# GpSimd's indirect DMAs in two expert layers, placed one or two slots apart

## The reference

```python
x = x + 0.5 * ffn0(layernorm(x))          # one 128x128 projection
x = x + linear_attention(layernorm(x))
x = x + 0.5 * ffn0(layernorm(x))
x = x + 0.5 * expert_layer(layernorm(x))  # <- the change is in this layer
x = x + attention_one_head(layernorm(x))
x = x + 0.5 * expert_layer(layernorm(x))  # <- and in this one

def expert_layer(src):                    # 16 heads of 8, 4 experts, ff 512
    q, k, v = src @ Wq + bq, src @ Wk + bk, src @ Wv + bv
    x = layernorm(src + softmax(q k^T / sqrt(8)) v @ Wo + bo)
    key = floor(x @ router_w + router_b) mod 4
    ff = relu(x @ W1[key] + b1[key]) @ W2[key] + b2[key]   # each token: one expert
    return layernorm(x + ff)
```

## Time and profile before

| what | value |
|---|---|
| time, three runs | 1491.17, 1488.88, 1481.77 us, median 1488.88 |
| the profiled execution, from its first to its last instruction | 1560.5 us |
| busy TensorE, VectorE, ScalarE, GpSimd | 1172.4, 944.3, 819.0, 691.4 us |
| mean granted clock of TensorE | 0.829 |
| chain that ended last | PE 53%, DVE 14%, issue 9%, DMA 7% |
| indirect DMAs on GpSimd | 64 scatters, 64 gathers, 48 weight transfers |

### The profile page before, as it was taken

One profiled execution on the slowest core, in us unless ns is written; L12 is line 12 of the kernel. 1 busy time (PEld: TensorE's weight loads), 2 busy tenths in 40 slices (PEclk: granted clock), 3 DMA queues, 4 the chain that ended last, 5 costly groups with the idle time before them and its releaser, 6 DMA issues.

```text
span 1560.5 us, 30073 instructions
## 1 busy us (share of the span) xinstructions
PE 1172.4 (75%) x10624; PEld 759.1 (49%) x10624; DVE 944.3 (61%) x2991; ACT 819.0 (52%) x1850; POOL 691.4 (44%) x679
## 2 busy tenths in 40 slices
PE   4899999874466987988886676467779888987753
PEld 3666766562133645644554564332326545644553
DVE  5477777664467656667526885556667566663231
ACT  4666555452165756765662343224557657754532
POOL 5335345465122454454427676442133544543352
PEclk8799999975588978979987988756869879887977
DMA  8000000002222433343112110202234433432133
GB/s 250 2 2 1 2 2 2 2 1 81 84 83 76 134 108 118 117 137 126 45 53 71 41 50 22 71 21 72 74 102 134 125 108 117 125 106 84 37 99 104
DMA packets 116340, 116.72 MB, mean 75 GB/s; under 512 B 9288, under 2 KB 100040, under 8 KB 116040
## 3 DMA queue, kind: packets, MB, share of 16 engines
q1 hardware_dynamic: 101488, 74.84, 15.4%
q0 software_dynamic: 11008, 36.81, 7.2%
q10 hardware_dynamic: 3696, 3.15, 0.7%
HBM read 73.01 MB, written 42.15 MB: 74 GB/s over the span
## 4 chain that ended last, share of the span: by engine, by line
PE 53%; DVE 14%; issue 9%; DMA 7%; ACT 6%; SPq 4%; POOL 4%; another core or an unknown queue 3%; ACTq 0%; POOLq 0%; DVEq 0%
PE bank L1657 7%; PE bank L1695 7%; PE bank L1672 6%; PE bank L1716 6%; DVE NM L2276 3%; DMA scr_m<-MH 2%; SPq L741 2%; PE bank L1904 2%; PE bank L1480 2%; PE bank L1745 2%; PE bank L1734 2%; PE bank L1806 2%; PE bank L1722 1%; PE bank L1422 1%
## 5 line engine op out<-in xcount | busy, mean ns | idle before, releaser
L2276 DVE TENSOR_REDUCE NM<-bank 128x2 f32<-128x512 f32 x512 | 340.1, 685 | 233.0 <-PE bank L1722 195.4
L1244 ACT ACTIVATE PBS<-bank 128x512 f32<-128x512 f32 x512 | 300.0, 604 | 263.5 <-PE bank L1716 222.3
L1716 PE MATMUL bank<-QS,KS 50*128 50x256 bf16 x1024 | 201.4, 300 | 129.1 <-DVE NM L2276 64.3
L874 POOL TENSOR_TENSOR rs<-ve,half 128x4 f32<-128x4 f32 x88 | 90.0, 1023 | 434.3 <-DVE ve L2187 329.6
L1722 PE MATMUL bank<-KS,QS 48*128 48x256 bf16 x1024 | 210.7, 310 | 27.0 <-DVE NM L2276 17.1
L1716 PEld LDWEIGHTS bank<-QS,KS 50*128 50x128 bf16 x1024 | 66.4, 98 | 261.6 <-issue 153.2
L1695 PE MATMUL bank<-PBS,V 128*32 128x256 f32 x2048 | 163.9, 446 | 1.4 <-ACT PBS L1244 1.4
L983 POOL DMA_INDIRECT scr_x<-XS,POS x64 | 63.9, 998 | 82.5 <-DVE POS L2242 63.5
L1722 PEld LDWEIGHTS bank<-KS,QS 48*128 48x128 bf16 x1024 | 66.0, 99 | 55.8 <-DVE NM L2276 40.6
L1695 PEld LDWEIGHTS bank<-PBS,V 128*32 128x32 f32 x2048 | 59.2, 121 | 63.8 <-issue 35.1
L1218 ACT ACTIVATE HB<-bank,W 128x128 f32<-128x128 f32 x256 | 74.5, 396 | 24.1 <-PE bank L1657 19.9
(11 more groups left out here) (319 smaller groups left out, 2672.8 us busy)
## 6 DMA issues: line engine op xcount, KB each, us to landing
QS<-scr_q SPq DMA_DIRECT2D x64, 192.0 KB
KS<-scr_k SPq DMA_DIRECT2D x56, 192.0 KB
XD<-scr_x SPq DMA_DIRECT2D x16, 448.0 KB
scr_q<-PQ SPq DMA_DIRECT2D x32, 192.0 KB, 2.1
scr_k<-PQ SPq DMA_DIRECT2D x28, 192.0 KB, 2.1
scr_q<-PQ SPq DMA_DIRECT2D x32, 128.0 KB, 1.9
scr_y<-YB SPq DMA_DIRECT2D x16, 256.0 KB
scr_k<-PQ SPq DMA_DIRECT2D x28, 128.0 KB, 1.9
```

Of the source, the lines that this page charges most:

```text
L874: pool.tensor_tensor(rs_[:, :], ve_[:, :], half[:, 0:ve_.shape[1]], ALU.pow).then_inc(rstd_sem, 1)
L1244: act.activation(PB[i % PB_SLOTS][:, :, :], bank[1 + i % 2][:, :].rearrange("p (k t) -> p k t", k=2), ACT.Exp).then_inc(A.e, 1)
L1716: last_s = pe.matmul(bank[1 + s % 2][:, k * T:(k + 1) * T], KS[1 - par][r, b, s // 2, k * P:(k + 1) * P], QS[1 - par][r, b, s // 2, :], st ...
L2276: dve.tensor_reduce(NM[:, 2 * b + qt, h:h + 3:2], bank[3 + i % 2][:, :].rearrange("p (u t) -> p u t", u=2), AX_X, ALU.max, negate=True).th ...
```

## The change

The table `AT` gets a slot for each indirect DMA: the four scatters in slots 2, 4, 6 and 8 (before: all in slot 0), the four gathers in 9, 11, 13 and 14 (all in slot 1), the three weight transfers in 16, 17 and 18 (all in slot 7). In steps 1 to 7 each of them now waits for the scores of the slot before its own (`beside_scores`). What follows the gathers moves back: acc 15 to 18, acc_stats and acc_moments 18 to 19 and 20, acc_rstd 15 to 21, en (20, 23) to (23, 25), eg 24 to 26, x_add 26 to 29. `TAIL` and `START` repeat their single slots, so their steps are as before. Line numbers of the changed kernel are higher by up to 12.

```diff
-... "acc": 15, "acc_stats": 18, "acc_moments": 18, ... "x_add": 26, ...
-... "en": (20, 23), ... "scatter": 0, "gather": 1, "v1": 4, "weights": 7, ... "acc_rstd": 15, "xs": 20, "eg": 24
+... "acc": 18, "acc_stats": 19, "acc_moments": 20, ... "x_add": 29, ...
+... "en": (23, 25), ... "scatter": (2, 4, 6, 8), "gather": (9, 11, 13, 14), "v1": 4, "weights": (16, 17, 18), ... "acc_rstd": 21, "xs": 20, "eg": 26
...
+                    def beside_scores(i):
+
+                        if att and n < PAIRS:
+                            pool.wait_ge(A.s, c * 32 + (i - 32))
+
                     for i in slots:
...
-                        if exp and i == slot["scatter"]:
+                        if exp and i == slot["scatter"][0]:
                             pool.wait_ge(E.pos, c - 2)
...
-                            for t in range(TP):
+                        for t in range(TP):
+                            if exp and i == slot["scatter"][t]:
+                                beside_scores(i)
                                 pool.indirect_dma_start(
                                     out=scr_x, out_offset=bass.IndirectOffsetOnAxis(ap=POS[other][:, t:t + 1], axis=0),
                                     in_=XS[other][:, t, :], in_offset=None).then_inc(E.scattered, 16)
...
```

More of the change, by code:

```diff
@@ L49 @@
 AT = {"x_stats": 0, "x_moments": 0, "max1": 4, "div2": 7, "div3": 8, "z": 12, "z_stats": 12, "z_moments": 13, "q_mid":
[2 rows of a table removed]
[2 rows of a table added]
       8, "x_turn": 7, "q": 9, "anT": 9, "k": 11, "wo": 12, "v": 12, "xd0": 14, "xd1": 14, "up": (15, 17, 19, 21, 23,
       25, 27), "down": (18, 19, 21, 24, 27, 28, 30), "m0T": 16, "turn0": 19, "turn1": 24, "ranks": 30, "y": (3, 5),
[1 row of a table removed]
-      (15, 17, 19, 21, 23, 25, 27), "x_rstd": 0, "scatter": 0, "gather": 1, "v1": 4, "weights": 7, "rest1": (6, 12),
-      "z_rstd": 15, "rest2": (15, 15), "acc_rstd": 15, "xs": 20, "eg": 24, "yr": 24}
[1 row of a table added]
+      (15, 17, 19, 21, 23, 25, 27), "x_rstd": 0, "scatter": (2, 4, 6, 8), "gather": (9, 11, 13, 14), "v1": 4, "weights": (16, 17, 18), "rest1": (6, 12),
+      "z_rstd": 15, "rest2": (15, 15), "acc_rstd": 21, "xs": 20, "eg": 26, "yr": 24}
 TAIL = {"x_stats": 1, "x_moments": 3, "max1": 1, "div2": 4, "div3": 6, "z": 12, "z_stats": 13, "z_moments": 14, "q_mid":
@@ L64 @@
         "yt": 15, "qev": 7, "kev": 10, "anc": 8, "vev": 21, "zn": (16, 19), "en": (20, 22), "xt0": 13, "xt1": 16,
-        "relu": (15, 17, 19, 21, 23, 25, 27), "x_rstd": 0, "scatter": 2, "gather": 3, "v1": 5, "weights": 3, "rest1":
+        "relu": (15, 17, 19, 21, 23, 25, 27), "x_rstd": 0, "scatter": (2, 2, 2, 2), "gather": (3, 3, 3, 3), "v1": 5, "weights": (3, 3, 3), "rest1":
         (8, 13), "z_rstd": 13, "rest2": (15, 18), "acc_rstd": 16, "xs": 20, "eg": 22, "yr": 29}
@@ L74 @@
          "yt": 7, "qev": 9, "kev": 11, "anc": 9, "vev": 12, "zn": (17, 18), "en": (20, 23), "xt0": 8, "xt1": 16, "relu":
-         (15, 17, 19, 21, 23, 25, 27), "x_rstd": 0, "scatter": 0, "gather": 1, "v1": 3, "weights": 6, "rest1": (6, 12),
+         (15, 17, 19, 21, 23, 25, 27), "x_rstd": 0, "scatter": (0, 0, 0, 0), "gather": (1, 1, 1, 1), "v1": 3, "weights": (6, 6, 6), "rest1": (6, 12),
          "z_rstd": 15, "rest2": (15, 15), "acc_rstd": 15, "xs": 20, "eg": 24, "yr": 24}
@@ L985, in step @@
                                     in_=XS[other][:, t, :], in_offset=None).then_inc(E.scattered, 16)
-                        if fin and i == slot["gather"]:
+                        if fin and i == slot["gather"][0]:
                             pool.wait_ge(E.ystored, 32 * (c - 3))
@@ L989, in step @@
                                 pool.wait_ge(E.acc, c - 4)
-                            for t in range(TP):
+                        for t in range(TP):
+                            if fin and i == slot["gather"][t]:
+                                beside_scores(i)
                                 pool.indirect_dma_start(
@@ L1002, in step @@
                                                ALU.add).then_inc(A.vcopied, 1)
-                        if exp and i == slot["weights"]:
+                        if exp and i == slot["weights"][0]:
                             if later(c - 3):
                                 pool.wait_ge(E.yused, 2 * (c - 3))
-                            for k in range(OVER):
+                        for k in range(OVER):
+                            if exp and i == slot["weights"][k]:
+                                beside_scores(i)
                                 pool.indirect_dma_start(
```

## The result

The changed kernel takes 1513.76 us (median of 4 runs, 1508.90 to 1521.69), the kernel before 1488.18 (4 runs). The ratio is 1.0202, 95% interval 1.0167 to 1.0236: slower by 25.6 us. The forecast was 12 us slower. Its sign held, and its range up to 1516; its size did not.

The account below looks back on a forecast made before the run. TensorE held 53% of the chain, VectorE 14%, GpSimd 4%; bursts counted 0 in timed runs. Median 1488.9 plus 7 (fourth scatter) plus 5 (weights) gave 1500.9, say 1500 us; range 1455 to 1516, likeliest case 1489 to 1508.

Parts of the forecast that it names:

- the stall: VectorE's late waits beside bursts of eight DMAs, steps 4 to 7: 35 to 47 us, taken as the recorded execution's alone.
- The rival that wanted the 41 us in the timed runs: Bursts of eight also stall timed runs, so breaking them up gains 41 us there: 1460 us; chance 0.25.
- At most two indirect DMAs then stand together: On GpSimd's queue after the change: bursts shrink to two indirect DMAs, three with the weights; timed runs 0.
- the third rival: GpSimd runs behind, DMAs stand together again behind their waits, all else is covered: 1489 +- 6 us; chance 0.06.
- Fourth scatter: Behind the first qkr, steps 3 to 6 of two layers: transposes of slot 14 come 1.70 us late, +7 us.
- I take half: Half the scatter's delay is absorbed as VectorE catches up: 0.9 us a step, +7 us; bounds 0 and +15.
- Clock: New TensorE waits at slots 14 and 23, 1 to 2 us long, cause no clock fall: counted 0.
- Weights: Transfers behind both parts of PQ, steps 3 to 6, eight times: 0.6 us late a step, +5 us.
- nearly as fast as alone: Weight transfers beside PQ's stores get some four fifths of the bytes, so land near the 8.4 us alone.
- equal sharing: Weights and PQ's stores share engines evenly in time: weights 3.6 us late, +29 us; as rival 1513, chance 0.20.
- Gathers and VectorE: Later gathers, AC at slot 18 and its moved statistics delay nobody: 0, with 3 us either way.
- A span of 1526: Recorded execution of the changed kernel: 1560.5 - 47 + 12 = 1526 us, while the median stays near 1500.

Follow-up runs that it names:

- same_order: Changed kernel with every indirect DMA a slot apart but in the old order: scatters 0 to 3, gathers 3 to 6, weights 7 to 9; 1483.56 us, ratio 0.9990.
- the second record of before: Another recorded run of the kernel before, written with the changed kernel's tables, all places as before and no new waits; 1478.28 us, span 1476.5.
- scatter_early: Changed kernel with the scatters in slots 2 to 5, ahead of the first qkr; the rest stays as changed; 1507.83 us, ratio 1.0088.
- after_w14: Changed kernel with only the three weight transfers moved, to slot 14 ahead of both parts of PQ; 1504.60 us, ratio 1.0136.
- weights_14: Changed kernel with the scatters in slots 2 to 5 and the three weight transfers in slot 14, ahead of PQ; 1493.94 us, ratio 1.0049.
- z_first: Changed kernel with scatters in slots 2 to 5, gathers in 9, 10, 11, 13, z_rstd in 14, weights in 15; 1506.87 us, ratio 1.0140.
- acc_17: z_first with VectorE's AC one slot earlier, 17 for 18; 1498.40 us, ratio 1.0078.

## Why the prediction was right and wrong

- **Bursts and the recorded execution.** That the stall is not in the timed runs was right, and it decided the sign. That bursts of eight make it in a recorded execution was wrong: the stall of the earlier trace rows is in one record and in none of the later ones, with bursts of four, seven and eight; a timed run's time is its record's span plus 1.8 us there. What the first record suffered from stays open. The rival that wanted the 41 us in the timed runs is out. "At most two indirect DMAs then stand together" did not come true either: three do in step 4 of the changed kernel, and same_order shows how little the table's slots spread them, as the third rival had it.
- **Fourth scatter.** The lateness was right (1.70 us; measured 1.6 to 2.3 in eight steps, 15.1 together). The step that failed is "I take half": nothing of it was absorbed. I had VectorE catch up during the wait, but it gets its scores from TensorE: its waits for them rose from 165.1 us in the second record of before to 193.2. 7 should have been 15, the bound.
- **Clock.** The second step that failed: "I count 0, and a fall would double them", with waits "shorter than the 2.7 us idle" as the reason. The fall came, in seven of eight steps, behind waits of 1.6 to 2.3 us, so one row with 2.7 us was no reason. TensorE's busy time grew by 9.9 us against the second record of before and by 5.5 against that of same_order: the term was 5.5 to 9.9 and not 0.
- **Weights.** +5 was put in; 1.4 us of waits stand in the profile. Not because they were on time: with XD early they cost 13.4 us of waits. I summed as if a delay in slot 14 and one in slot 23 were paid apart; the first buys time for the second. My choice "nearly as fast as alone" was wrong too: 10.6 us from their issue or 581.28 - 570.49 = 10.8 from PQ's end, between the 8.4 alone and the 12.5 from PQ's end that equal sharing gave (596.3 - 583.84). The Trainium skill ("DMA: Bandwidth & Descriptors", section "SWDGE vs HWDGE vs iDMA") has the queues served in turn, which by packet size gave a term near 0; the waits of scatter_early, 13.4 / 8 = 1.7 us a step, decide against that reading of it.
- **Gathers and VectorE.** VectorE's places cost 0, as said (1.0006). The gathers cost 0.7% by themselves, by the waits through z_rstd, a queue that I did not go along: in the changed kernel that wait is not there, since the weights no longer stand ahead of it.
- **Profile.** A span of 1526 was forecast, 1516.0 came, 2.2 above the median.

Measured, the 24.9 us of the eight steps are 15.0 of idle time, about as much as the waits for XD (15.1), and 9.9 of busy time, the clock's and perhaps in part the difference of two records. So of the forecast's 7 + 5 the 7 became 15, the 5 about 1, and the clock's 0 became 5.5 to 9.9. That 24.9 comes so near the 25.6 us between the medians is partly luck: the same two records differ by another 14.6 us outside these steps.

## What to carry to other kernels

Before an instruction is moved on an in-order queue, write down what it now stands behind and what that waits for; here one scatter behind one wait for ScalarE cost 0.9 to 1.4% (after_w14 against weights_14 and against the kernel before), and the kernel that kept the order lost nothing. Look in the trace, too, whether slots of a table become distances in time. A delay in an engine that all others take turns with is to be counted in full and, where it leaves TensorE idle for about 2 us in a dense stretch, with half-speed time likely behind it. When a recorded execution is 5% longer than the timed ones, get a second record before a term is read from the difference.

## What the runs showed of the hardware

- An addition of VectorE with both inputs in SBUF (AC, 0.68 us) took 3.82 us in six steps of z_first when it started beside three additions of GpSimd in a row, and 0.68 again in acc_17 when it ran beside DMA issues. The Trainium skill ("SBUF — State Buffer", section "Who interferes with whom") says that a VectorE instruction with two SBUF inputs contends with a GpSimd instruction that reads SBUF, since the second input comes through the shared read interface, and calls the shared ports an exclusive lock. The trace agrees, and shows more, since AC ended only after three such instructions had.
- Three GpSimd transfers of weights took 8.4 us alone (until the DMA engines stood idle) and 10.6 us beside the stores of SP's queue (scatter_early, until TensorE went on).
- A wait of TensorE of 1.6 to 2.3 us between dense matmuls was followed by a granted clock of 0.50 in seven of eight steps of the changed kernel (3.4 us long, once 6.8) and in five of eight of after_w14.
